# Softmax sums in an attention kernel: the second partial sum joined by an adding DMA, the reciprocal taken in PSUM, values stored by heads

## The reference

```
x = L0_attn_x                                    # 1 x 2048 x 1024
xn = _layernorm(x)
qkv = xn @ attn_qkvw + attn_qkvb                 # q, k, v: 32 heads x 2048 x 32
scores = einsum('bhqd,bhkd->bhqk', q, k) * scale
probs = softmax(scores, axis=-1)
ctx = einsum('bhqk,bhkd->bhqd', probs, v)
x = x + (ctx @ attn_ow + attn_ob) + ffn(xn)      # ffn: top 16 of 64 experts of rank 8
```

## Time and profile before

| | us |
|---|---|
| median of the runs (lowest, highest of 3) | 2536.3 (2536.12, 2541.24) |
| the profiled execution | 2535.3 |
| its span | 2533.5 |
| busy: PE, POOL, DVE, ACT | 2489.4, 1627.9, 1509.8, 1207.8 |
| granted TensorE clock, mean of the span | 0.994 of full |
| attention stage, about | 702 to 2260 |

### The profile page before, as it was taken

The page is one execution under the profiler, slowest core; times in us unless marked ns, Lnnn a source line. Parts: engine busy times, 40 slices in busy tenths (PEclk is TensorE's granted clock), DMA queues, the critical chain, the costliest instruction groups (busy, mean ns, idle before and its releaser), DMA issues. The chain is left out here.

```text
span 2533.5 us, 34397 instructions
## 1 busy us (share of the span) xinstructions
PE 2489.4 (98%) x12888; PEld 1632.0 (64%) x12888; DVE 1509.8 (60%) x2524; ACT 1207.8 (48%) x2295; POOL 1627.9 (64%) x556
## 2 busy tenths in 40 slices
PE   7999999999989999999999999999999999989999
PEld 6888888888845555555555555555555555548887
DVE  8511110103568788878888878888878887622221
ACT  3211111110046666666666767666767676771000
POOL 0101111221068999999999999999999999962111
PEclk9999999999989999999999999999999999999999
DMA  4233335323177777877777787777787787664332
GB/s 166 92 125 124 115 115 163 109 79 117 58 183 148 165 153 156 168 150 159 165 157 152 165 167 147 162 165 153 155 169 150 153 171 152 129 167 141 114 104 88
DMA packets 174685, 359.23 MB, mean 142 GB/s; under 512 B 90384, under 2 KB 115472, under 8 KB 143504
## 3 DMA queue, kind: packets, MB, share of 16 engines
q0 software_dynamic: 22752, 165.69, 33.1%
q1 hardware_dynamic: 151792, 191.70, 26.6%
HBM read 127.42 MB, written 63.70 MB: 75 GB/s over the span
## 5 line engine op out<-in xcount | busy, mean ns | idle before, releaser
L1109 DVE TENSOR_REDUCE part_max<-ps_b 128x1 f32<-128x512 f32 x1984 | 1213.9, 681 | 274.8 <-PE ps_b L982 274.7
L933 POOL TENSOR_TENSOR psum_p<-psum_p,probs 128x2048 f32<-128x2048 f32 x253 | 1181.2, 4669 | 52.3 <-ACT probs L1095 42.2
L1095 ACT ACTIVATE probs<-ps_b 128x512 f32<-128x512 f32 x1920 | 970.8, 624 | 357.2 <-PE ps_b L972 352.5
L972 PE MATMUL ps_b<-qp,kp 97*128 97x512 f32 x1344 | 548.0, 412 | 0.0
L982 PE MATMUL ps_b<-kp,qp 96*128 96x512 f32 x1344 | 536.5, 401 | 7.2 <-DMA qp<-qk_scr 6.6
L1000 PE MATMUL ps_b<-probs,vh 128*32 128x512 f32 x3840 | 464.4, 598 | 0.5 <-ACT probs L1095 0.5
L972 PEld LDWEIGHTS ps_b<-qp,kp 97*128 97x128 f32 x1344 | 252.3, 188 | 224.5 <-issue 135.8
L321 POOL TENSOR_TENSOR wlo<-wraw,whi 128x1024 fp32r<-128x1024 f32 x21 | 50.3, 2397 | 417.7 <-ACT whi L462 417.7
L972 PE MATMUL ps_b<-qk 97*128 97x512 f32 x704 | 290.3, 416 | 5.3 <-PEq L82 5.2
L982 PEld LDWEIGHTS ps_b<-kp,qp 96*128 96x128 f32 x1344 | 256.7, 191 | 56.2 <-DVE part_max L1109 17.2
L982 PE MATMUL ps_b<-qk 96*128 96x512 f32 x640 | 254.3, 397 | 0.0
(11 more groups left out here) (107 smaller groups left out, 2427.2 us busy)
## 6 DMA issues: line engine op xcount, KB each, us to landing
psum_q<-probs POOLq DMA_DIRECT2D x158, 1024.0 KB, 7.7
qk<-qk_scr SPq DMA_DIRECT2D x66, 256.0 KB, 7.1
qk_scr<-ehi SPq DMA_DIRECT2D x16, 1024.0 KB, 3.9
qk_scr<-elo SPq DMA_DIRECT2D x16, 1024.0 KB, 6.8
kp<-qk_scr SPq DMA_DIRECT2D x63, 256.0 KB, 4.2
qp<-qk_scr SPq DMA_DIRECT2D x63, 256.0 KB, 7.9
wraw<-wcat SPq DMA_DIRECT2D x21, 512.5 KB, 7.5
craw<-cz_scr SPq DMA_DIRECT2D x14, 768.0 KB, 4.9
```

The costliest lines, as they stand in the source:

```text
L933: pool.tensor_tensor(acc[:, :], first[:, :], tile(h, t)[:, :], ALU.add).then_inc(pool_done, 1)
L972: pe.matmul(ps[:, st_bank(n), :], kp[s][0:PACK + 1, t * P:(t + 1) * P], qp[s][0:PACK + 1, b * NQ:(b + 1) * NQ], start=True, stop=True).the ...
L1095: act.activation(tile(h, t)[:, b * NQ:(b + 1) * NQ], ps[:, st_bank(n), :], ACT.Exp, scale=SCALE).then_inc(exp_done, 1)
L1109: dve.tensor_reduce(part_max[hn % 2][:, tn, b:b + 1], ps[:, ring_bank(u), :], AX_X, ALU.max) \
```

## The change

A head's sums take another way. After the add of tile 2 of head h, GpSimd issues one more adding DMA (`merge(h-1)`), which adds `psum_p` of head h-1 onto its `psum_q`. It waits for GpSimd's own last add and for the landing of the fifth DMA of head h-1. TensorE then multiplies only `psum_q` with ones, and does so in tile 8 of the next head, when the sixth DMA has landed. ScalarE's copy and SP's nine small DMAs go. VectorE takes the reciprocal of the sums in place, in their PSUM bank, in four parts of 128 columns in tiles 9 to 12, and multiplies each with the raw context (`normalise` moves from GpSimd to VectorE and from two heads later to one). The bank of the sums is held until the last multiply: the ring becomes a list of idle banks, worked out ahead, with three for maxima in that time. SP stores a head's context one head earlier, behind the load of values and ahead of `load_negmax`. Values lie in memory by heads, [32, 128, 16, 32]: a head's load is 128 runs of 2048 bytes, and the stores become runs of 512 bytes. The last head's own sums stay as they were.

```diff
-SUMS_AT, RECIPROCAL_AT = 6, 9
+MERGED_AFTER = 2
+SUMS_AT = 8
+DIVIDE_AT = SUMS_AT + 1
+GIVEN_BACK_AT = DIVIDE_AT + QB - 1
...
-                sp.dma_start(v_scr[t * P:(t + CHUNK) * P, half * NQ:(half + 1) * NQ].rearrange("(j p) c -> p j c", p=P),
-                             v_out[:, CHUNK * (q % 2):CHUNK * (q % 2 + 1), :]).then_inc(stored[q % 2], 16)
+                heads = slice(half * NQ // HD, (half + 1) * NQ // HD)
+                sp.dma_start(v_scr[heads, :, t:t + CHUNK, :].rearrange("h p v d -> p h (v d)"),
+                             v_out[:, q % 2, :, :, :].rearrange("p h v d -> p h (v d)")).then_inc(stored[q % 2], 16)
...
+                if t == GIVEN_BACK_AT and h >= 1:
+                    ring_order.append(("given back", h - 1, 0, 0))
...
             elif kind == "sum":
-                eng.wait_ge(sums_taken, h + 1)
+                eng.wait_ge(ctx_ready, QB * (h + 1))
...
-                sp.dma_start(vh[s][:, :, :], v_scr[:, h * HD:(h + 1) * HD].rearrange("(t p) c -> p t c", p=P)) \
+                sp.dma_start(vh[s][:, :, :], v_scr[h, :, :, :]) \
...
                     if h + 2 < HEADS:
                         load_keys(h + 2)
-                    if h >= 2:
-                        store_ctx(h - 2)
...
                     if h + 2 < HEADS:
                         sp.wait_ge(pv_done, TT * h + 4)
                         load_queries(h + 2)
-                    invert_sums(h - 1)
                     if h + 2 < HEADS:
                         load_values(h + 2)
+                    store_ctx(h - 1)
                 if h < LAST:
                     load_negmax(h + 1)
...
-            def normalise(h):
-                pool.wait_ge(raw_done, h + 1)
-                pool.wait_ge(recip_loaded, 16 * QB * (h + 1))
-                wait(pool, ctx_stored[h % 2], 16 * QB * (h // 2))
-                pool.tensor_tensor(out_ctx[h % 2][:, :], raw_ctx[h % 3][:, :], recip_b[:, :], ALU.mult) \
-                    .then_inc(ctx_ready, 1)
...
+            def merge(h):
+                pool.wait_ge(pool_done, pool_count(h, POOL_TILES[-1]))
+                pool.wait_ge(chained[h % 2], merged_count(h) - 16)
+                pool.sem_inc(cleared, 1)
+                pool.dma_start(psum_q[h % 2][:, :], psum_p[h % 2][:, :], accum_op=ALU.add) \
+                    .then_inc(chained[h % 2], 16)
...
             for h in range(HEADS):
-                if h >= 2:
-                    normalise(h - 2)
                 for t in LAST_POOL_ORDER if h == LAST else POOL_ORDER:
-                    if h == LAST and t == LAST_POOL_TILES[-1]:
-                        normalise(LAST - 1)
                     if t in chain_tiles(h):
                         chain(h, t)
                     else:
                         add(h, t)
+                    if t == MERGED_AFTER and h >= 1:
+                        merge(h - 1)
...
-                pe.wait_ge(chained[h % 2], chain_count(h, CHAIN_TILES[-1]))
-                sum_of(ring_bank(u), psum_q[h % 2], True, False)
-                pe.wait_ge(pool_done, pool_count(h, POOL_TILES[-1]))
-                sum_of(ring_bank(u), psum_p[h % 2], False, True).then_inc(sum_ready, 1)
+                pe.wait_ge(chained[h % 2], merged_count(h))
+                sum_of(ring_bank[u], psum_q[h % 2], True, True).then_inc(sum_ready, 1)
...
-            def reciprocal(h):
-                dve.wait_ge(sums_spread, 16 * QB * (h + 1))
-                wait(dve, recip_stored, 16 * h)
-                dve.reciprocal(recip_q[:, :], sums_q[:, :]).then_inc(recip_done, 1)
+            def reciprocal(h, part):
+                bank = ps[:, ring_bank["sum", h, 0, 0], part * P:(part + 1) * P]
+                if part == 0:
+                    dve.wait_ge(sum_ready, h + 1)
+                dve.reciprocal(bank, bank).then_inc(recip_done, 1)
+
+            def normalise(h, part):
+                c = slice(part * P, (part + 1) * P)
+                dve.wait_ge(recip_done, QB * h + part + 1)
+                if part == 0:
+                    dve.wait_ge(raw_done, h + 1)
+                    wait(dve, ctx_stored[h % 2], 16 * QB * (h // 2))
+                dve.tensor_tensor(out_ctx[h % 2][:, c], raw_ctx[h % 3][:, c], ps[:, ring_bank["sum", h, 0, 0], c],
+                                  ALU.mult).then_inc(ctx_ready, 1)
...
-                    for u in maxima_at(h, t):
-                        take_max(*u)
-                    if t == RECIPROCAL_AT and h >= 1:
-                        reciprocal(h - 1)
+                    ahead = maxima_at(h, t)
+                    for b in range(max(QB, len(ahead))):
+                        for u in ahead[b:b + 1]:
+                            take_max(*u)
+                        if h >= 1 and 0 <= t - DIVIDE_AT < QB:
+                            if b == 1:
+                                reciprocal(h - 1, t - DIVIDE_AT)
+                            if b == 3:
+                                normalise(h - 1, t - DIVIDE_AT)
...
-    v_scr = nc.dram_tensor("v_scr", [T, D], F32, kind="Internal").ap()
+    v_scr = nc.dram_tensor("v_scr", [HEADS, P, TT, HD], F32, kind="Internal").ap()
```

More of the change, by code:

```diff
@@ L644, in _ @@
                 dve.wait_ge(stored[j // CHUNK], QK_STORED + 16 * g)
-                dve.tensor_tensor(v_out[:, j, :], ps[:, j, :], vbias[:, half * NQ:(half + 1) * NQ], ALU.add) \
+                dve.tensor_tensor(v_out[:, j // CHUNK, :, j % CHUNK, :], ps[:, j, :].rearrange("p (h d) -> p h d", d=HD),
+                                  vbias[:, half * NQ:(half + 1) * NQ].rearrange("p (h d) -> p h d", d=HD), ALU.add) \
                     .then_inc(v_taken, 1)
@@ L738, in attend @@
                     ring_order.append(("sum", h - 1, 0, 0))
+                if t == GIVEN_BACK_AT and h >= 1:
+                    ring_order.append(("given back", h - 1, 0, 0))
                 if t == TRANSPOSED_AT and h < LAST:
                     ring_order.append(("flip", h + 1, 0, 0))
-        ring_order.append(("sum", LAST, 0, 0))
-        ring_place = {u: n for n, u in enumerate(ring_order)}
-        maxima_until, ready_until = [0], [0]
+        ring_bank, ring_before, maxima_until, ready_until = {}, {}, {}, {}
+        idle = [(RING_BANK + n, None) for n in range(RING_BANKS)]
+        maxima, ready = 0, 0
         for u in ring_order:
-            maxima_until.append(maxima_until[-1] + (u[0] == "max"))
-            ready_until.append(ready_until[-1] + (u[0] != "sum"))
-        def ring_bank(u):
-            if u == ("sum", LAST, 0, 0):
-                u = ("sum", LAST - 1, 0, 0)
-            return RING_BANK + ring_place[u] % RING_BANKS
-        all_maxima = maxima_until[-1]
-        unused = [RING_BANK + (ring_place["sum", LAST - 1, 0, 0] + i) % RING_BANKS for i in (1, 2)]
+            if u[0] == "given back":
+                u = ("sum", *u[1:])
+                idle.append((ring_bank[u], u))
+                continue
+            ring_bank[u], ring_before[u] = idle.pop(0)
+            maxima += u[0] == "max"
+            ready += u[0] != "sum"
+            maxima_until[u], ready_until[u] = maxima, ready
+            if u[0] != "sum":
+                idle.append((ring_bank[u], u))
+        ring_bank["sum", LAST, 0, 0] = ring_bank["sum", LAST - 1, 0, 0]
+        all_maxima = maxima
+        unused = [RING_BANK + n for n in range(RING_BANKS)
+                  if RING_BANK + n not in (ring_bank["sum", LAST, 0, 0], ring_bank["flip", LAST, 0, 0])]
         first_wide = 4 * TT * WIDE_FROM[0] + 4 * WIDE_FROM[1]
@@ L1056, in _ @@
             last_sums(TT - 1)
-            bank = ring_bank(("sum", LAST, 0, 0))
+            bank = ring_bank[("sum", LAST, 0, 0)]
             pe.wait_ge(chained[LAST % 2], chain_count(LAST, LAST_CHAIN_TILES[-1]))
@@ L1071, in take_sums @@
                 act.wait_ge(sum_ready, h + 1)
-                wait(act, sums_spread, 16 * QB * h)
-                act.activation(sums_b[:, :], ps[:, ring_bank(("sum", h, 0, 0)), :], ACT.Copy).then_inc(sums_taken, 1)
+                act.activation(sums_b[:, :], ps[:, ring_bank[("sum", h, 0, 0)], :], ACT.Copy).then_inc(sums_taken, 1)
             def wait_tile(h, t):
@@ L1098, in _ @@
                         take_raw(h - 1)
-                    if t == SUMS_AT and h >= 1:
-                        take_sums(h - 1)
             take_raw(LAST)
```

51 lines of the change are left out of this document (18 added, 33 removed).

## The result

| | before | after |
|---|---|---|
| median of the runs, us (lowest, highest of 4) | 2537.19 (2536.12, 2541.24) | 2690.14 (2688.11, 2693.1) |
| the profiled execution, us | 2535.3 | 2688.1 |

The ratio is 1.0598, with a 95% interval of 1.0586 to 1.0611. The change costs 153 us. The prediction said 2632 us, 95 above this measured time of the kernel before, and its range ended at 2680.

What follows compares the result with a forecast made beforehand. TensorE was taken as the bound, GpSimd close behind at 96.8%. GpSimd's head becomes 45.6 of work + 2.9 + 2.3 + 0.7 = 51.5 us, 3.1 more; 30 heads (93) plus 4 on 2535.3 give 2632 us, range 2560 to 2680.

Steps and rivals of the forecast that it cites:

- The mechanism: GpSimd, issuing in order, waits for two DMA landings around merge; its head grows by 3.1 to 51.5 us.
- the late row: load_negmax on SP, now behind four context stores: delays the next head's first product by 0, or 1 us, inside GpSimd's wait.
- (a): GpSimd before merge's issue: waits for the landing of the previous head's tile 14 DMA, 2.9 us a head.
- (b): GpSimd before tile 6's DMA: waits for tile 3's, queued behind merge's and landing after 12.1 us; 2.3 a head.
- (c): Query and value loads beside the adding DMAs lengthen landings: 0.7 us a head, between 0 and 2.2.
- the forecast's own spread: (c) from 0 to 1.5, second transfer's 2.3 give or take 0.6: 50.2 to 52.9 a head, 2593 to 2676 us.
- Rival 4: Full contention, tile 14's landing 9.0 and the two transfers 13.6: 53.9 us a head, 2704 us; chance 0.07.
- VectorE's pairs: Two tile pairs a head, each with two reciprocals (0.99 us) and two multiplies, last 7.08 to 7.81 us instead of 5.80.
- TensorE's loop: TensorE's head: 48.36 less 0.86 plus 2.6 for VectorE's longer pairs, 50.1 us, under GpSimd's 51.5, so nothing added.
- The values' layout: Stores of v_scr become rows of 512 B, loads runs of 2 KB; the stores' effect was put at nothing.
- The end: Last head on GpSimd goes from 35.7 to 40.1 us, 4 more.
- TensorE's 0.86 a head: Half of a head's 16 sum records on TensorE go, saving 0.86 us a head if TensorE stays the bound.

Runs made afterwards that it cites:

- 9: Kernel before with values by heads, sixth DMA after tile 4, sums in tile 10, reciprocal in 14, old way out, row issued ahead of late stores: 2542.19 us, 1.0015.
- 10: Same kernel as 9 with one number changed, the sixth adding DMA after tile 2 instead of tile 4: 2713.42 us, 1.0675.
- 13: Changed kernel with the row of negated maxima issued ahead of the context stores on SP: 2689.58 us, 1.0596.
- 17: Changed kernel with loads of keys, queries and values cut to a sixteenth of their columns from the third head on: 2628.51 us, 1.0357.
- 1: Changed kernel without the sixth adding DMA, TensorE summing both accumulators again in tile 8: 2687.72 us, 1.0582.
- 8: Kernel before with the transpose of the next head's maxima one tile later, so the row goes out beside tile 12's DMA: 2726.57 us, 1.0738.
- 2: Kernel before with the sixth adding DMA alone after tile 2, sums in tile 8, small reciprocal in 11, old way out: 2691.62 us, 1.0605.
- 4: Kernel before with the values' layout by heads alone: 2538.0 us, 0.9999.
- 6: Changed kernel without the sixth adding DMA, tile 12's DMA issued after the add of tile 13: 2634.78 us, 1.038.
- 5: Changed kernel without the sixth adding DMA, the row of negated maxima issued ahead of the four context stores: 2658.34 us, 1.0489.
- 16: Kernel 9 with the multiply of the raw context on VectorE instead of GpSimd, both operands in on-chip memory: 2656.36 us, 1.047.

## Why the prediction missed: direction right, one term too small

**The mechanism** is the one forecast: merge makes GpSimd wait for two landings a head, and its chain sets the pace. Experiments 9 and 10 show what such waits cost, 13 that the late row adds nothing to them, and 17 that shorter waits shorten the head by as much. The measured share of GpSimd is 87.2, forecast 89.

**(a), the wait before merge**, was put at 2.9, without the loads. It is 3.3 with them (7.88 + 0.60 - 5.14) and 2.7 with short loads (17).

**(b), two transfers in a row**, was put at 12.1 us to the second landing, a wait of 2.3. In the last two heads, which have no loads beside them, it is 11.8. With short loads the mean is 12.63, a wait of 2.8: there the second lands after 11.8 us in some heads and after 13.3 to 14.0 in others, even where the short loads had landed before. What lengthens it in those heads stays open.

With the second transfer started only when the first had landed it would have been 13.6, and the last two heads show 11.8. So the rule of the Trainium skill (DMA: Bandwidth & Descriptors, Two DMAs through the same engine are not ordered), that descriptors of one queue are pipelined, agrees with the trace.

**(c), the loads on top, is the step that failed**: "I take 0.7, between 0 and 2.2." Experiment 17 gives 2.0: the two waits are 7.5 with the loads (3.3 + 4.2) and 5.5 with a sixteenth of them (2.7 + 2.8). The bounds held, but the value was near the low one, and the forecast's own spread stopped at 1.5. The argument for the small value was that part of the loads would fall on idle engines between the transfers. Part of them does. SyncE's queue after, and the hardware queue's row (packets, MB, share of the 16 engines) for the window 1210 to 1212.5, in which merge's DMA is issued:

```profile
1205.75 2.41 SPq L847 DMA_DIRECT2D qp<-qk_scr  x3
1208.20 0.76 SPq L852 DMA_DIRECT2D vh<-v_scr  x1
```

```profile
q1 hardware_dynamic: 127, 0.49, 89.3%
```

The loads go out while tile 14's DMA is in flight. Around merge's issue, when that DMA has landed and no packet of merge's has started, they hold 89% of the engines' time. But they are too much for that gap. Worked out from the packets of heads 1 to 29, as means over the 16 engines: the loads take 1.0 us before tile 14's landing and 1.6 in the gap that follows, until 1.45 us after merge's issue, where merge's first packet starts in the last two heads. Another 1.5 come from there to the second landing. So some 1.6 us fall on idle engines, as the forecast said, and 2.5 don't. Both landings are lengthened, where the forecast reckoned with one.

With the measured terms the head is 45.6 + 3.3 + 4.2 = 53.1, and the trace has 53.36. Against the forecast's 51.5, the loads make 1.3 of the difference, the pair without them 0.5, and tile 14's landing without them takes 0.2 off. Rival 4, full contention (9.0 and 13.6), gave 53.9 and 2704: the nearest case, at a chance of 0.07. Its 13.6 is nearly the measured 13.97, but for another reason: it let the second transfer begin after the first, and in the last two heads it doesn't.

**VectorE's pairs**, 7.08 to 7.81 forecast, are 7.20 to 7.50, and the reciprocal 0.96 (forecast 0.99). The prediction's estimate of 8.3 ns a column, from the repeat count of 8 that the Trainium skill (VectorE: DVE Perf Modes, First, the fixed hardware budget) gives, is not borne out: 0.96 us for 128 columns, less 0.153 for one, is 6.4 a column. Its loop of 51.0 by that estimate was also a slip; the same sum gives 50.3.

**TensorE's loop** was put at 50.1 and is 53.41 - 0.86 = 52.5, by experiment 1. Of the 2.4 between, 2.0 are the late row, which the forecast called "0, or 1 us". It reckoned with the stores ahead of the row and not with the adding DMA in flight, behind which it lands (8). This second slip had no effect on the time, as the forecast rightly placed it inside GpSimd's wait (13); but the two loops end within a microsecond of each other, and so experiments 1 and 2 each look like the whole cause. Mending either alone gives nothing.

**The rest.** The values' layout is worth nothing, as forecast (4). The end cost 4, as forecast. TensorE's 0.86 a head are there, in the pair of the sums: 7.80 is 5.80 + 0.86 + 1.15 of wait.

No version beat the kernel before. The nearest with the sixth DMA, 9, is 0.15% above it, and by then GpSimd has no time left to give. What stays open is how the 2.0 us a head of experiment 17 divide between keys, queries and values, which were not tried singly.

## What to carry to other kernels

An engine that issues its work in order pays every landing that it waits for in full, unless it has as much work of its own in between: count that work, and for each wait take the landing as it is with every load that is then in flight, once for every transfer. When two loops lie within a microsecond of each other, undoing one part alone shows nothing, and each part alone shows everything; try both before naming a cause. Where the next stage waits for a small DMA, look at what large transfer is in flight at that moment, and not only at its own queue: here the small one landed when the large one had.

## What the runs showed of the hardware

- A row of 8 KB lands in 1.8 us in most heads when no adding DMA is in flight (6). When one of 1 MB is, on another queue, the means are 4.9 to 5.6 (5, 8, 1), and in 29 of 31 heads of 8 the row lands 0.15 to 0.18 behind it.
- Adding DMAs of 1 MB: 6.8 us alone; of two issued 0.62 apart, in heads without loads, the second lands 11.8 after the first's issue.
- With TensorE busy for 1.19 of 4 us its mean granted clock was 0.54 of full in that window, 0.61 in the next 4 us, all of them busy, and 1.00 in the 4 after (8).
- An issue on GpSimd takes 0.61 us from the next add; in kernel 9 the one at 1220.77 took 0.75, its record 1.51 instead of 0.87, and the add behind it 5.38 instead of 4.6 to 4.9.
- A multiply on VectorE with both operands in the on-chip memory took 4.35 us beside an add of GpSimd's and ended 0.55 after it (16). The Trainium skill (SBUF — State Buffer, SBUF: two separate sides) says that a VectorE operation with two such inputs and a GpSimd one that reads there exclude each other for a whole instruction; this trace agrees.
